# Loop entry of a cross-attention and mixture-of-experts kernel: bias add moved to VectorE, two weight chunks split in another way, one exponential and one load moved

## The chip, the cores and the metric

One core of a Trainium2 chip runs one program. The metric is the device time of that core in microseconds (us); before the change it is 419.9 us, the median of three runs (419.73 to 420.04).

## The reference, cut to what matters

```python
x = x + xattn(layernorm(x), ctx, mask)     # x: 2 x 1024 x 256; ctx: 2 x 77 x 256; 16 heads of 64
x = x + moe_ffn(layernorm(x))              # 9 experts, hidden 704, the two best of each token

def xattn(q, ctx, mask):
    qh, kh, vh = split(q @ Wq), split(ctx @ Wk), split(ctx @ Wv)
    attn = softmax(where(mask, -max, qh @ kh.T / 8))
    return merge(attn @ vh) @ Wo + bo
```

## The kernel before, in words

The 2048 tokens are 16 tiles of 128. The program has three parts: a prologue on the context alone, a loop of 16 steps (one token tile each, with later stages of earlier tiles beside it), and the experts.

**Prologue.** For each pair of heads m (8 pairs) TensorE makes keys (`keys(m)`), multiplies them with the query weights (`key_side(m)`, L554 to L564, into a ring of four PSUM banks), and makes values (`value_side(m)`, L571). ScalarE and VectorE take each result out of PSUM as a float16 part and its remainder: `a_high`/`a_low` for the key side, `v_even`/`v_odd` for the values. `key_side(m)` waits until `a_low` has read the banks that it reuses: `at_least(pe, a_lo_ok, 2 * m - 2)` (L556), so `key_side(3)` waits for both instructions of `a_low(1)`. The order of each engine's instructions is written out by hand. TensorE's is ... `key_side(2)`, `keys(7)`, `key_side(3)`, `value_side(0)`, `value_side(1)`, `key_side(4)`, `value_side(2)`, the transpose of token tile 0, and so on (L805 to L824). VectorE's begins (L1506 to L1510):

```python
a_low(0)
dve.wait_ge(xall_in[0], 16)
stats1_of(0, 2)      # statistics of token tiles 0 and 1, from x_all
aggregate1(0)
for m in range(1, 3):
    a_low(m)
```

GpSimd makes the reciprocal standard deviation of these tiles (`rstd_first`), ScalarE normalises them.

**Loads.** SyncE issues all of them from one queue in program order (L400 to L445): the context, the key weights in three parts, the first quarter of the query weights; then it waits for the second part of the key weights and issues token tiles 0 and 1 (`load_x_all(0)`, 256 KB), the second quarter of the query weights, the constants, the first half of the value weights (`load_wv(0)`, 512 KB), the rest of the query weights, the second half of the value weights, the mask, tiles 2 and 3, the bias, the output weights, three quarter-chunks of expert weights, and all other token tiles.

**Steps 0 and 1 (the loop entry).** TensorE does `scores(n)`, the transpose of tile n+1 and `make_b(g)` for g = 0, 1, 2 (step 0) and 3, 4 (step 1). `make_b` multiplies the values with Wo, so that the loop needs one product less; its ten results use PSUM banks 3 to 6 in turn, and `make_b(2)` waits until `b_low(0)` has read banks 3 and 4 (L588). For g = 0 it also adds the bias bo by a product with an identity, into the first 77 rows. ScalarE's `b_high` and VectorE's `b_low` split each result. `scores(2)` begins when `b_low(4)` is done (L749).

**Expert weights.** 36 chunks of 128 x 1088 elements go through three staging slots. `w_high(c)` on ScalarE scales a chunk in place and then casts it to float16 (two passes); `w_low(c)` on GpSimd writes the remainder. `w_direct(c)` casts and scales in one pass, and `w_rest(c)` on VectorE makes scale and remainder in one instruction; before, this pair is used for late chunks only. SyncE loads chunk c when chunk c-3 is done (L432). Its queue is in order, so `turn_x(3)` (a DMA transpose of tile 3 that needs GpSimd's `norm_low(3)`) stands ahead of `load_x(4)` and of chunks 6 and 7.

**Step 2.** ScalarE does `p_high(0)`, two `w_high`, then `normalise(4)` (which waits for `load_x(4)`), `exp(2)`, `norm_high(4)`; step 3 begins with `p_high(1)`. VectorE's `sums(2)`, `p_low(1)` and `residual(0)` follow from them, and `project(1)` on TensorE needs `residual(0)`.

Of the kernel before, what the change touches and what calls it, by code (L numbers as in the profile page):

```python
# [71 lines left out]
def build(nc, x, ctxT, mask, wq, wk, wv, wo, bo, wt, gate, gbias, consts, out):  # L72
    with ExitStack() as ctx:
# [6 lines left out]
        def sems(name, n):  # L80
            return [sem(f"{name}{k}") for k in range(n)]
# [176 lines left out]
        con_in, bc_in, ctx_in, mask_in = (sem(n) for n in ("con_in", "bc_in", "ctx_in", "mask_in"))  # L258
        wk_in, wq_in, wv_in = sems("wk_in", 3), sems("wq_in", 4), sems("wv_in", 2)
        wo_in, xall_in, half_mm, bo_in = sems("wo_in", 2), sems("xall_in", 3), sem("half_mm"), sem("bo_in")  # L260
        setup = sem("setup")
        cpy = sem("cpy")
        mask_ok = sem("mask_ok")
# [31 lines left out]
        LAG_OUT, LAG_X1, LAG_XN2, LAG_G = 2, 3, 4, 5  # L295
        W_STEP = 2
        W_PRE = 4
        WARM, WARM_IDS, WARM_HALF, WARM_OUT, WARM_X0 = 30, 28, 18, 6, 4

        X_PE = 3  # L300
# [97 lines left out]
        def _(sp):  # L398
# [15 lines left out]
            for g in range(4):  # L414
                sp.dma_start(wq_sb[:, 2 * g:2 * g + 2],
                             wq[2 * g * P:2 * (g + 1) * P].rearrange("(m p) n -> p m n", p=P)).then_inc(wq_in[g], 16)
                if g == 0:
                    sp.wait_ge(wk_in[1], 16)
                    load_x_all(0)
                if g == 1:  # L420
                    sp.dma_start(con[:], consts).then_inc(con_in, 16)
                    load_wv(0)
            load_wv(1)
            sp.dma_start(mask32, mask).then_inc(mask_in, 16)
            load_x_all(1)
# [118 lines left out]
        def _(pe):  # L544
# [41 lines left out]
            def make_b(g):  # L586

                at_least(pe, b_lo_ok, (0, 0, 2, 6, 6)[g])  # L588
                for half in range(2):
                    pe.wait_ge(wo_in[half], 16)  # L590
                    pe.wait_ge(v_half[half], PAIRS)
                even, odd = b_terms(2 * g, 0), b_terms(2 * g + 1, 1)
                if g == 0:
                    pe.wait_ge(bo_in, 16)
                rest = b_terms(2 * g, 1)
                assert len(even) == len(odd)
                for i in range(len(even)):
                    end = i == len(even) - 1
                    more = rest or g == 0
                    mm = b_product(*even[i], start=(i == 0), stop=(end and not more))  # L600
                    if end:
                        mm.then_inc(half_mm if more else b_mm, 1)
                    mm = b_product(*odd[i], start=(i == 0), stop=end)
                    if end:
                        mm.then_inc(b_mm, 1)
                    if g == 0 and end:
                        pe.wait_ge(half_mm, 1)
                        for b in range(B):
                            mm = pe.matmul(b_bank(0)[0:J, b], con[:, C_ID:C_ID + J], bo_b[:], start=False, stop=(b == B - 1),
                                           skip_group_check=True)  # L610
                        mm.then_inc(b_mm, 1)
                if rest:
                    pe.wait_ge(half_mm, 2)
                    for i in range(len(rest)):
                        mm = b_product(*rest[i], stop=(i == len(rest) - 1))
                    mm.then_inc(b_mm, 1)
# [285 lines left out]
        def _(act):  # L902
# [16 lines left out]

            def b_high(g):  # L920
                act.wait_ge(b_mm, 2 * g + 2)
                for k in (2 * g, 2 * g + 1):
                    act.activation(b_hi[:, :, B_CHUNKS[k], :], b_bank(k), ACT.Copy, scale=SP_B).then_inc(b_hi_ok, 1)

# [18 lines left out]
            def w_high(c):  # L943

                act.wait_ge(w_in[c % SLOTS], c // SLOTS * 16 + 16)
                act.activation(stage[:, c % SLOTS, :], stage[:, c % SLOTS, :], ACT.Copy, scale=SP_W).then_inc(w_sc_ok, 1)  # L946
                act.wait_ge(w_sc_ok, c + 1)
                act.activation(w_chunk(c, 0), stage[:, c % SLOTS, :], ACT.Copy).then_inc(w_hi_ok, 1)  # L948

            def w_direct(c):  # L950
# [37 lines left out]

            def step(n):
                if n == 0:  # L990
                    w_high(0)
                    x_high(1)
                    b_high(0)
                    w_high(1)
                    exp(0)
                    normalise(2)
                    b_high(1)
                    b_high(2)
                    return
                if n == 1:  # L1000
                    w_high(2)
                    x_high(2)
                    normalise(3)
                    w_high(W_PRE - 1)
                    norm_high(3)
                    b_high(3)
                    exp(1)
                    b_high(4)
                    return
                if on(n, LAG_OUT):  # L1010
                    p_high(n - LAG_OUT)
                if on(n, LAG_XN2):
                    normalise2(n - LAG_XN2)
                if n == W_STEP:
                    act.wait_ge(b_mm, NCH)
                if on_w(n) and w_place(w_at(n)) < 4:
                    act.wait_ge(stats1, NT - 3 if w_place(w_at(n)) == 0 else NT)
                if n == NT - 1:
                    gate_copy(n - LAG_G)
                if on_w(n):  # L1020
                    w_high(w_at(n))
                    w_high(w_at(n) + 1)
                if n == LAG_G:
                    act.wait_ge(zero_out, 64)
                if on(n, LAG_G) and n != NT - 1:
                    gate_copy(n - LAG_G)
                if on(n, -2):
                    normalise(n + 2)
                if n == NT - 1:
                    w_high(4 * EARLY + 2)  # L1030
                if on(n, 0):
                    exp(n)
                if on(n, -2):
                    norm_high(n + 2)
# [118 lines left out]
        def _(dve):  # L1153
# [7 lines left out]
            def v_odd(m):  # L1161
# [2 lines left out]
                dve.tensor_copy(vz[rows, m % 3, :, j0:j0 + J],  # L1164
                                ps[rows, V_BANKS[m % 3], 0:B * J].rearrange("p (b j) -> p b j", b=B)).then_inc(v_half[1], 1)

            def b_low(g):
                for k in (2 * g, 2 * g + 1):
                    c = B_CHUNKS[k]
                    dve.wait_ge(b_hi_ok, k + 1)  # L1170
                    dve.scalar_tensor_tensor(out=b_lo[:, :, c, :], in0=b_bank(k), scalar=SP_B, in1=b_hi[:, :, c, :],
                                             op0=ALU.mult, op1=ALU.subtract).then_inc(b_lo_ok, 1)
# [104 lines left out]

            def w_rest(c):

                dve.wait_ge(w_lo_ok, c)  # L1280
                dve.wait_ge(w_hi_ok, c + 1)
                dve.scalar_tensor_tensor(out=w_chunk(c, 1), in0=stage[:, c % SLOTS, :], scalar=SP_W, in1=w_chunk(c, 0),
                                         op0=ALU.mult, op1=ALU.subtract).then_inc(w_lo_ok, 1)
# [153 lines left out]
            def step(n):  # L1437
                if n == 2:
                    b_low(4)
                if on(n, 1):  # L1440
                    sums(n - 1)
                if n == 1:
                    b_low(1)
                    b_low(2)
                    dve.wait_ge(xall_in[2], 16)
                    stats1_of(4, 6)
                if on(n, LAG_OUT):
                    p_low(n - LAG_OUT)
                if on(n, LAG_X1):
                    residual(n - LAG_X1)  # L1450
                if on(n, 0):
                    maxima(n)
                if on(n, LAG_X1):
                    stats(n - LAG_X1)
                if on(n, 0):
                    shift(n)
                if on(n, LAG_X1):
                    aggregate(n - LAG_X1)
                if n in (0, 1):
                    x_low(n + 1)  # L1460
                if n == 0:
                    b_low(0)
                if n == 1:
                    b_low(3)
                    stats1_of(6, 8)
                    aggregate1(2)
                    dve.wait_ge(bc_in, 32)
                if X_PAIR <= n + 4 < NT:
                    stats1_of(n + 4, n + 5)
                if on(n, LAG_G):  # L1470
                    logits(n - LAG_G)
                    pick(n - LAG_G)
# [175 lines left out]
        def _(pool):  # L1648
# [56 lines left out]
            def step(n):  # L1705
                if on_w(n - 1):
                    w_low(w_at(n - 1) + 1)
                if n == 0:
                    w_low(0)
                    w_low(1)  # L1710
                if on(n, 1):
                    norm(n - 1)
                if n == 1:
                    w_low(2)
                    rstd_first(2)
                    w_low(W_PRE - 1)
# [122 lines left out]
```

## Time and profile before

| | |
|---|---|
| median of three runs | 419.9 us (419.73 to 420.04) |
| profiled execution | 419.24 us, its span 417.4 us |
| TensorE busy | 400.7 us (96% of the span) |
| VectorE, ScalarE, GpSimd busy | 276.3, 253.6, 253.5 us |
| chain that ended last, by engine | TensorE 52%, issue 16%, DMA 13%, VectorE 7% |

PE is TensorE's matmuls, PEld its weight loads, DVE VectorE, ACT ScalarE, POOL GpSimd, SP or SPq SyncE and its queue. Times are from the start of the span. The loop entry lies between 22.3 us and about 58 us of the span, the rest of the loop reaches to about 157 us, and the experts follow. Busy shares are averages over parts with different limits, so what the change is worth has to be read in its own stretch.

### The profile page before, as it was taken

The page shows a single profiled execution, that of the slowest core. Times are in us where ns is not written, and L with a number is a line of the kernel's source. Part 1 is how long each engine was busy: PE and PEld are TensorE (multiplying, and loading weights), DVE is VectorE, ACT ScalarE, POOL GpSimd, SP SyncE. Part 2 cuts the span into 40 slices and gives each one's busy share as a digit, 9 for nine tenths or more (in the row PEclk, how much of TensorE's full clock was granted, in tenths as well). Part 3 has the DMA queues.
Part 4 walks back from the last instruction along what each step waited for, and adds up shares of the span by engine and source line. Part 5 has one row for each costly group of instructions (what it writes and reads, how often), then busy time and mean ns, then how long its engine had stood idle before and what let it go on. Part 6 is the DMA issues. An engine that isn't in the chain of part 4 may idle for free.

```text
span 417.4 us, 10090 instructions
## 1 busy us (share of the span) xinstructions
PE 400.7 (96%) x3150; PEld 301.6 (72%) x3150; DVE 276.3 (66%) x668; ACT 253.6 (61%) x444; POOL 253.5 (61%) x214
## 2 busy tenths in 40 slices
PE   8999999999999999899999999999999999999991
PEld 7777676777777777777677777777777777777780
DVE  1777968999999999989889754434444444444330
ACT  3759789999999996735655434444444444444430
POOL 6536789999999999263345543545444444454232
PEclk9999999999999999999999999999999999999996
DMA  7993287777676787247789779999988998889842
GB/s 226 343 359 108 71 217 185 209 202 209 197 200 209 191 216 209 89 126 192 123 146 142 142 132 146 125 146 144 137 140 139 140 142 140 138 141 149 121 65 35
DMA packets 113584, 67.73 MB, mean 162 GB/s; under 512 B 88064, under 2 KB 106880, under 8 KB 113536
## 3 DMA queue, kind: packets, MB, share of 16 engines
q1 hardware_dynamic: 105856, 56.60, 59.8%
q0 software_dynamic: 7680, 10.49, 16.4%
q8 instruction: 30, 0.49, 0.5%
q14 instruction: 18, 0.15, 0.1%
HBM read 36.23 MB, written 9.96 MB: 111 GB/s over the span
## 4 chain that ended last, share of the span: by engine, by line
PE 52%; issue 16%; DMA 13%; DVE 7%; POOL 5%; POOLq 4%; ACT 2%; SPq 1%; DVEq 0%; ACTq 0%
PE ps L847 14%; PE ps L676 10%; PE ps L646 10%; DMA out_rows<-work,idx_all 9%; PE ps L867 6%; PE ps L659 3%; POOL work L1739 3%; POOLq L1748 3%; PE ps L642 2%; DMA w_all<-in_wv 2%; PE ps L583 2%; PE ps L548 1%; PE ps L691 1%; DVE work L1230 1%; DVE work L1221 1%
## 5 line engine op out<-in xcount | busy, mean ns | idle before, releaser
L847 PE MATMUL ps<-w_all,work 128*128 x960 | 150.3, 313 | 0.5 <-DVE work L1477 0.4
L847 PEld LDWEIGHTS ps<-w_all,work 128*128 128x128 f16 x960 | 93.6, 98 | 46.9 <-issue 1.2
L1760 POOL DMA_INDIRECT out_rows<-work,idx_all x40 | 64.2, 1605 | 101.4 <-ACT work L1109 91.8
L1545 DVE SCALAR_TENSOR_TENSOR work<-ps,work 128x352 f32<-128x352 f32 x80 | 41.3, 523 | 66.1 <-PE ps L847 65.9
L867 PE MATMUL ps<-w_all,work 128*128 x681 | 80.8, 273 | 0.1
L867 PEld LDWEIGHTS ps<-w_all,work 128*128 128x128 f16 x681 | 66.3, 98 | 10.8 <-issue 0.4
L1673 POOL TENSOR_TENSOR w_all<-stage,w_all 128x1088 f16<-128x1088 f32 x31 | 70.1, 2260 | 5.5 <-ACT w_all L948 5.5
L1088 ACT ACTIVATE work<-ps 128x352 f32<-128x352 f32 x80 | 36.7, 462 | 50.7 <-PE ps L847 50.7
L1094 ACT ACTIVATE work<-work 128x704 f16<-128x704 f32 x39 | 30.8, 790 | 58.5 <-DVE work L1545 58.5
L1739 POOL DMA_INDIRECT work<-xn_rows,idx_all x40 | 42.6, 1064 | 27.9 <-issue 10.4
L646 PE MATMUL ps<-w_all 128*128 128x462 f16 (+1 forms) x288 | 57.4, 336 | 0.0
L676 PE MATMUL ps<-w_all,work 128*128 128x256 f16 x320 | 53.5, 273 | 2.4 <-DVE work L1230 1.7
L646 PEld LDWEIGHTS ps<-w_all 128*128 128x128 f16 x288 | 27.9, 97 | 22.0
L676 PE MATMUL ps<-work 128*128 128x256 f16 x160 | 43.6, 273 | 0.0
L1678 POOL TENSOR_TENSOR work<-work 128x1232 f32<-128x1232 f32 x16 | 36.0, 2251 | 2.3 <-DVE work L1225 2.3
L676 PEld LDWEIGHTS ps<-w_all,work 128*128 128x128 f16 x320 | 30.4, 98 | 8.0 <-DVE work L1240 4.3
L946 ACT ACTIVATE stage<-stage 128x1088 f32<-128x1088 f32 x31 | 34.2, 1104 | 3.0 <-DMA stage<-in_wt 2.6
L948 ACT ACTIVATE w_all<-stage 128x1088 f16<-128x1088 f32 x31 | 34.4, 1111 | 1.0
L1552 DVE TENSOR_TENSOR work<-work 128x640 f16<-128x640 f32 x39 | 31.9, 818 | 0.0
L1551 DVE TENSOR_TENSOR work<-work 128x64 f16<-128x64 f32 x39 | 8.8, 227 | 30.9 <-ACT work L1094 30.8
L1221 DVE TENSOR_REDUCE work<-work 128x16 f32<-128x1232 f32 x16 | 22.8, 1423 | 7.5 <-ACT work L969 7.5
L1208 DVE TENSOR_REDUCE work<-ps 128x6 f32<-128x462 f32 (+1 forms) x48 | 25.1, 574 | 1.0 <-PE ps L646 1.0
(162 smaller groups left out, 530.5 us busy)
## 6 DMA issues: line engine op xcount, KB each, us to landing
stage<-in_wt SPq DMA_DIRECT2D x36, 544.0 KB, 4.3
work<-in_x SPq DMA_DIRECT2D x30, 128.0 KB, 2.5
out_rows<-work SPq DMA_DIRECT2D x18, 128.0 KB, 2.4
xn_rows<-work SPq DMA_DIRECT2D x18, 128.0 KB, 2.5
w_all<-in_x SPq DMA_DIRECT2D x1, 1536.0 KB, 14.1
work<-work SPq DMA_TRANSPOSE x78, 3.6
w_all<-in_wq SPq DMA_DIRECT2D x4, 256.0 KB, 6.1
w_all<-in_wv SPq DMA_DIRECT2D x2, 512.0 KB, 7.4
```

The costliest lines, as they stand in the source:

```text
L646: mm = pe.matmul(dst, lhs[:, par, k, :], rhs[:, k, b, h0 * J:h0 * J + w], start=False, stop=(k == KD - 1 and rhs is a_lo))
L676: mm = pe.matmul(ps[:, 6, 0:D], lhs[:, c, :], rhs[:, b, c, :], start=(c == 0 and n == 0), stop=(c == NCH - 1 and n == 2))
L847: mm = pe.matmul(ps[:, c, 0:half], xt[:, t % 2, block, :], weights(wbase + off, half), start=(k == 0 and n == 0), stop=(k == KD - 1 and n ...
L867: mm = pe.matmul(ps[:, Y_BANKS[t % 2], 0:D], lhs, weights(wbase + (pl * WC + W13C + c * D), D), start=(c == 0 and n == 0), stop=(c == HC - ...
L946: act.activation(stage[:, c % SLOTS, :], stage[:, c % SLOTS, :], ACT.Copy, scale=SP_W).then_inc(w_sc_ok, 1)
L948: act.activation(w_chunk(c, 0), stage[:, c % SLOTS, :], ACT.Copy).then_inc(w_hi_ok, 1)
L1088: act.activation(sg[:, t % 2, c * HID // 2:(c + 1) * HID // 2], ps[:, c, 0:HID // 2], ACT.Silu, scale=1.0 / SP_W).then_inc(silu_ok, 1)
L1545: dve.scalar_tensor_tensor(out=sg[:, t % 2, cols], in0=ps[:, 2 + c, 0:HID // 2], scalar=1.0 / SP_W, in1=sg[:, t % 2, cols], op0=ALU.mult, ...
L1673: pool.tensor_tensor(w_chunk(c, 1), stage[:, c % SLOTS, :], w_chunk(c, 0), ALU.subtract).then_inc(w_lo_ok, 1)
L1678: pool.tensor_tensor(e3, e3, rr[:, i % 2].unsqueeze(2).to_broadcast([P, HEADS, J]), ALU.mult).then_inc(norm_ok, 1)
L1739: pool.indirect_dma_start(out=xg[:, t % 2], out_offset=None, in_=xn2_rows[0:K1 * P, :] if t < NF1 else xn2_rows, in_offset=bass.IndirectOf ...
L1760: pool.indirect_dma_start(out=acc, out_offset=bass.IndirectOffsetOnAxis(ap=idx_all[:, t:t + 1], axis=0), in_=yb[:, t % 2], in_offset=None, ...
```

## The change: what it does

- The bias product on TensorE goes. VectorE adds the bias in PSUM (`add_bias`) after the first result of `make_b(0)`, and `b_high(0)` waits for it.
- Chunks 0 and 1 are split by `w_direct` on ScalarE and `w_rest` on VectorE, in place of `w_high` and `w_low`. `w_direct(1)` stands ahead of `b_high(0)`.
- In step 2 `exp(2)` stands ahead of `normalise(4)`.
- `load_x_all(0)` is issued after `load_wv(0)`; the wait ahead of it stays where it was. VectorE's order in the prologue is unchanged.

```diff
@@ sync
                 if g == 0:
                     sp.wait_ge(wk_in[1], 16)
-                    load_x_all(0)
                 if g == 1:
                     sp.dma_start(con[:], consts).then_inc(con_in, 16)
                     load_wv(0)
+                    load_x_all(0)
@@ tensor, make_b
                 even, odd = b_terms(2 * g, 0), b_terms(2 * g + 1, 1)
-                if g == 0:
-                    pe.wait_ge(bo_in, 16)
                 rest = b_terms(2 * g, 1)
                 for i in range(len(even)):
                     end = i == len(even) - 1
-                    more = rest or g == 0
-                    mm = b_product(*even[i], start=(i == 0), stop=(end and not more))
+                    mm = b_product(*even[i], start=(i == 0), stop=(end and not rest))
                     if end:
-                        mm.then_inc(half_mm if more else b_mm, 1)
+                        mm.then_inc(half_mm if rest else b_mm, 1)
                     mm = b_product(*odd[i], start=(i == 0), stop=end)
                     if end:
                         mm.then_inc(b_mm, 1)
-                    if g == 0 and end:
-                        pe.wait_ge(half_mm, 1)
-                        for b in range(B):
-                            mm = pe.matmul(b_bank(0)[0:J, b], con[:, C_ID:C_ID + J], bo_b[:], start=False, stop=(b == B - 1),
-                                           skip_group_check=True)
-                        mm.then_inc(b_mm, 1)
@@ scalar
             def b_high(g):
                 act.wait_ge(b_mm, 2 * g + 2)
+                if g == 0:
+                    act.wait_ge(bias_ok, 1)
@@ scalar, w_high
-                act.wait_ge(w_sc_ok, c + 1)
+                act.wait_ge(w_sc_ok, c + 1 - W_REST)
@@ scalar, step
                 if n == 0:
-                    w_high(0)
+                    w_direct(0)
                     x_high(1)
+                    w_direct(1)
                     b_high(0)
-                    w_high(1)
                     exp(0)
                     normalise(2)
...
+                if n == W_STEP:
+                    exp(n)
                 if on(n, -2):
                     normalise(n + 2)
...
-                if on(n, 0):
+                if on(n, 0) and n != W_STEP:
                     exp(n)
@@ vector
+            def add_bias():
+                dve.wait_ge(bo_in, 16)
+                dve.wait_ge(b_mm, 1)
+                dve.tensor_tensor(b_bank(0)[0:J], b_bank(0)[0:J], bo_b[0:J].unsqueeze(1).to_broadcast([J, B, D]),
+                                  ALU.add).then_inc(bias_ok, 1)
@@ vector, step
                 if n == 1:
+                    w_rest(1)
                     b_low(1)
                     b_low(2)
...
                 if n == 0:
+                    add_bias()
+                    w_rest(0)
                     b_low(0)
@@ gpsimd, step
-                if n == 0:
-                    w_low(0)
-                    w_low(1)
                 if on(n, 1):
                     norm(n - 1)
                 if n == 1:
+                    pool.wait_ge(w_lo_ok, W_REST)
                     w_low(2)
```

## Rows read from the trace of the kernel before

**Rows 1.** Busy time by stretch: us, then each engine's busy us, granted clock, DMA share, GB/s
```profile
22.30:58.20 35.90, 34.50 (x243) 23.63 (x240) 27.30 (x58) 28.85 (x41) 22.59 (x19) 1.00 0.59 180
58.20:154.00 95.80, 95.79 (x731) 72.63 (x732) 90.06 (x217) 91.28 (x131) 93.84 (x86) 1.00 0.72 201
```

**Rows 2.** The chain of waits that ended last: start us, us, what
```profile
7.08 6.79 DMA w_all<-in_wv
14.00 1.29 PE ps L548 x8
...
28.20 1.09 PE ps L609 x4
29.29 4.52 PE ps L583 x40
...
50.46 2.39 DMA work<-in_x
...
58.21 3.45 PE ps L676 x30
```

**Rows 3.** TensorE in order of time, key_side(3) and value_side(0): start, us, idle before
```profile
12.34 0.79 PE L560 MATMUL ps<-w_all 64*128 64x154 f32 x8
14.00 1.29 PE L548 MATMUL ps<-w_all 128*128 128x154 f32 x8 [0.87 <-DMA w_all<-in_wv]
```

**Rows 4.** VectorE in order of time: the two statistics, and a_low(1)
```profile
10.04 0.74 DVE L1177 BATCH_NORM_STATS2 st_all<-w_all 128x6 f32<-128x256 f32 x2
...
10.91 0.83 DVE L1190 TENSOR_TENSOR w_all<-ps,w_all 128x308 f16<-128x308 f32 x2
```

**Rows 5.** SyncE's issues in order of time, around the load that moves
```profile
5.64 0.37 SPq L408 DMA_DIRECT2D w_all<-in_x  x1
...
7.08 0.43 SPq L411 DMA_DIRECT2D w_all<-in_wv  x1
7.56 0.98 SPq L415 DMA_DIRECT2D w_all<-in_wq  x2
```

**Rows 6.** DMA issues of the same stretch in turn: KB, us from issue to landing
```profile
w_all<-in_x SPq DMA_DIRECT2D x1, 256.0 KB, 3.0
...
con<-in_consts SPq DMA_DIRECT2D x1, 246.0 KB, 4.8
w_all<-in_wv SPq DMA_DIRECT2D x1, 512.0 KB, 6.8
w_all<-in_wq SPq DMA_DIRECT2D x1, 256.0 KB, 7.1
```

**Rows 7.** Busy time by stretch, with the rate of all transfers at the end
```profile
10.00:15.00 5.00, 4.13 (x36) 3.29 (x33) 3.60 (x12) 2.94 (x9) 2.18 (x7) 1.00 0.98 325
```

**Rows 8.** VectorE: x_low(1), b_low(0) (two instructions), and all five w_rest
```profile
27.91 0.41 DVE L1194 TENSOR_TENSOR w_all<-ps,w_all 128x256 f16<-128x256 f32 x1
...
29.95 1.29 DVE L1171 SCALAR_TENSOR_TENSOR work<-ps,w_all 128x512 f16<-128x512 f32 x2 [1.63 <-ACT w_all L923]
L1282 DVE SCALAR_TENSOR_TENSOR w_all<-stage,w_all x5: 1279/1283/1289, 182.0 to 208.3; 128x1088 f16<-128x1088 f32 x5
```

**Rows 9.** ScalarE in order of time: b_high(0), normalise(4), the scaling pass of chunk 7
```profile
29.32 1.08 ACT L923 ACTIVATE w_all<-ps 128x512 f16<-128x512 f32 x2 [2.68 <-PE ps L609]
52.88 0.60 ACT L936 ACTIVATE work<-work,nmr_all,rstd_all 128x256 f32<-128x256 f32 x1 [2.65 <-DMA work<-in_x]
58.62 1.11 ACT L946 ACTIVATE stage<-stage 128x1088 f32<-128x1088 f32 x1 [0.34 <-DMA stage<-in_wt]
```

**Rows 10.** GpSimd in order of time: norm_low(3)
```profile
48.40 0.69 POOL L1702 TENSOR_TENSOR work<-work 128x256 f16<-128x256 f32 x1
```

**Rows 11.** TensorE's longest wait between 22 and 62 us: total, times, longest
```profile
PE ps L676 <- DVE work L1240: 0.7, 1, 0.7
```

**Rows 12.** Busy time by stretch after TensorE's last work, with the granted clock
```profile
408.30:410.60 2.30, 0.01 (x1) 0.00 (x0) 0.00 (x0) 0.47 (x1) 0.90 (x2) 1.00 0.47 57
412.00:417.40 5.40, 0.00 (x0) 0.00 (x0) 0.00 (x0) 0.00 (x0) 0.00 (x0) 0.50 0.21 24
```

More of the change, by code:

```diff
@@ L260, in build @@
         wo_in, xall_in, half_mm, bo_in = sems("wo_in", 2), sems("xall_in", 3), sem("half_mm"), sem("bo_in")
+        bias_ok = sem("bias_ok")
         setup = sem("setup")
@@ L297, in build @@
         W_PRE = 4
+        W_REST = 2
         WARM, WARM_IDS, WARM_HALF, WARM_OUT, WARM_X0 = 30, 28, 18, 6, 4
@@ L605, in make_b @@
                         mm.then_inc(b_mm, 1)
-                    if g == 0 and end:
-                        pe.wait_ge(half_mm, 1)
-                        for b in range(B):
-                            mm = pe.matmul(b_bank(0)[0:J, b], con[:, C_ID:C_ID + J], bo_b[:], start=False, stop=(b == B - 1),
-                                           skip_group_check=True)
-                        mm.then_inc(b_mm, 1)
                 if rest:
-                    pe.wait_ge(half_mm, 2)
+                    pe.wait_ge(half_mm, 1)
                     for i in range(len(rest)):
@@ L1278, in w_rest @@
             def w_rest(c):
-                dve.wait_ge(w_lo_ok, c)
+                at_least(dve, w_lo_ok, c)
                 dve.wait_ge(w_hi_ok, c + 1)
```

## The prediction, made before the changed kernel was run

> **What bounds the kernel now.** I read the busy shares by stretch first, then the chain of waits, then each engine in order of time where the change lies. From 58.2 to 154 us TensorE is busy 95.79 of 95.80 us [rows 1]: whatever reaches `project(1)`, its first work at 58.21 [rows 2], earlier or later moves the rest of the kernel by the same amount, as long as the other engines keep up. They have little room: VectorE, ScalarE and GpSimd are busy 94%, 95% and 98% of that stretch (90.06, 91.28, 93.84 of 95.80) [rows 1]. From 22.3 to 58.2 us TensorE is idle for 1.4 us [rows 1], of which one wait of 0.7 us stands at `project(1)`, for VectorE's `residual(0)` [rows 11]. Ahead of the loop it waits once more, 0.87 us for the value weights [rows 3]. So the sum to make is when `project(1)` starts after the change.
>
> **The load that moves, and who waits for it.** SyncE issues tiles 0 and 1 at 5.64, the value weights at 7.08 and the next quarter of the query weights at 7.56 [rows 5]. They land 3.0, 6.8 and 7.1 us later [rows 6], at 8.64, 13.87 (7.08 + 6.79 [rows 2]) and 14.66: in the order of issue, and from 10 to 15 us the DMA engines are 98% busy [rows 7]. After the change the value weights have 256 KB less ahead of them. The next 256 KB cost 14.66 - 13.87 = 0.8 us, so they land at about 13.1, when `key_side(3)` ends (12.34 + 0.79 = 13.13) [rows 3]. That alone would remove the 0.87 us.
>
> But the tiles now stand behind them. They have ahead of them and with them just the bytes that the value weights had before, and the issue is at the same place in the queue, so I take 13.9 us for their landing. Above, 14.7 (the place after). Below, if the transfers ran with no engine of the 16 late: the constants, one quarter of the query weights and the value weights were 246 + 256 + 512 = 1014 KB after the tiles' old landing at 8.64 [rows 6]; at 325 GB/s [rows 7] that is 3.2 us, so 11.8.
>
> The tiles' statistics are not off the path. VectorE's order is fixed: `a_low(0)` from 9.26, the two statistics from 10.04, their aggregation, and `a_low(1)` from 10.91 to 11.74 [rows 4]. The tiles were there at 8.64, 1.4 us ahead of need. Now VectorE stops ahead of the statistics until 13.9, with `a_low(1)` queued behind, and `key_side(3)` on TensorE waits for `a_low(1)` (L556). From landing to `key_side(3)` it is 11.74 - 10.04 = 1.70 us of VectorE plus two hand-overs of 0.05 us: 15.7 instead of 12.34. It takes 0.72 us (eight products in a chain; the next begins with that distance), and `value_side(0)` starts at 16.4 instead of 14.00 [rows 3]. So this edit costs 2.4 us (bounds: 0.3 with 11.8, 3.2 with 14.7; it is neutral with a landing at 11.5 and gains up to 0.87 ahead of 10.6). Everything of the prologue behind it (value sides, normalisation of tile 0, last key sides) hangs on this start and shifts with it. The mask and the later loads don't hang on it.
>
> The Trainium skill (DMA: Bandwidth & Descriptors, section Queues, rings and completion order) says that each DMA engine takes the descriptors of its ring in order, while the 16 engines finish independently. The landings in order of issue agree with it [rows 5, 6]; by it a transfer that is moved behind 512 KB can't pass them, and the sum would be the same.
>
> **Bias off TensorE.** The bias product is 1.09 us of chain, with 0.05 us ahead of it, at 28.20 [rows 2]: -1.1 us for `make_b(1)`. VectorE's add has no row. The nearest is half of `b_low` (512 elements from PSUM in 1.29 / 2 = 0.65 us [rows 8]); it could be 0.5 or 0.8, and I take 0.65.
>
> **Two chunks on VectorE.** Each `w_rest` is 1.28 us [rows 8]. In step 0 VectorE now does the bias add, 0.65, and `w_rest(0)`, 1.25, ahead of `b_low(0)`, 1.29. `x_low(1)` ended at 28.3 [rows 8]; with the shift of 2.4 it ends at 30.7, the add at 31.35, `w_rest(0)` at 32.6, `b_low(0)` at 33.9. TensorE leaves `make_b(0)` at 28.15 + 2.4 = 30.55 [rows 2] and would reach `make_b(2)` 2.7 later, at 33.3 (24 of the 40 products in the 4.52 us of [rows 2]), so it waits 0.6 us there. That is the price of these edits; with the add at nothing it would be none, and with 0.2 us more in each 1.0. `w_rest(1)` is hidden: `b_low(2)` ends near 39.1, and TensorE needs it at 39.7, behind `scores(1)`. On ScalarE `w_direct` saves two passes of 1.1 us; one lies in the wait of 2.68 us that stood ahead of `b_high(0)` [rows 9]. The other brings `exp(0)` forward, which VectorE can't use at once. GpSimd loses 4.5 us of work where it was mostly idle. At the end of `make_b(4)` the tail to `scores(2)` (`b_high(4)`, `b_low(4)`) stays; by the same walk it is 0.3 us shorter, since `sums(1)` and the statistics no longer crowd it.
>
> **The exponential.** In step 2 ScalarE waited 2.65 us for tile 4 [rows 9], which was issued at 50.46 and landed at 52.85 [rows 2], with `exp(2)` behind it; `sums(2)`, `p_low(1)` and `residual(0)` followed, and TensorE waited 0.7 us [rows 11]. With `exp(2)` ahead that wait goes: -0.7. What is late next is tile 4 itself: SyncE issues it behind `turn_x(3)`, and that waits for GpSimd's `norm_low(3)`, which ended at 49.1 [rows 10]. By the walk `b_high(3)` ends at 44.1, `b_low(3)` at 44.9, the statistics of tiles 4 to 7 at 45.8, and GpSimd is done with them, one chunk and `norm_low(3)` 4.9 us later, at 50.7: 1.6 later than before, and so are tile 4 and chunks 6 and 7. Chunk 7 already held ScalarE up for 0.34 us [rows 9]. By the walk ScalarE is 1.3 us late after chunk 7, when TensorE is 0.9 late, and `project(2)` waits 0.3 us for `residual(1)`. ScalarE has too little room to win it back.
>
> **Sum.** +2.4 (tiles) - 1.1 (bias) + 0.6 (`make_b(2)`) - 0.3 (tail) - 0.7 (exponential) + 0.3 (ScalarE) = +1.2 us. On the profiled execution, 417.4 of span and 1.8 around it, that is 419.2 + 1.2 = 420.4. The median of the runs stands 0.7 above that execution, so I expect 421.1.
>
> **Rivals.**
> *The tiles land early.* If no DMA engine is late as one was for the value weights, the landing is 11.8 and that edit costs 0.3, 2.1 less: 421.1 - 2.1 = 419.0, faster by 0.9. (Chunk 0 and tile 2 land no earlier and ScalarE would wait for them, but within the waits that TensorE has anyway.) With a landing before 10.6 it is 1.2 less again, about 418. The place is VectorE's wait ahead of the statistics; with a landing after 12.7 the change is slower than none. For it: the tiles' first transfer needed 3.0 us only, the constants 4.8. Against: the transfers at that place in the queue needed 6.8 and 7.1 [rows 6].
>
> *The clock falls in the new gap.* TensorE would be idle from 12.4 to 15.7, 3.3 us. At the end of the span the granted clock was still 1.00 (2.4 GHz) in the 2.3 us after the last product, and 0.50 (1.2 GHz) from 412 on [rows 12]. So the gap is longer than an idle time that can end at the lower level. What a fall costs has no row before the end: nothing at least, at most the 8.3 us of prologue left (14.00 to 22.34) once more; I take 1.6, since the work from 15.7 on is dense, and get 422.7. For it: the length of the gap. Against: the clock stays at 1.00 in every stretch until the end, and I can't tell how it looks at a gap with dense work on both sides.
> The Trainium skill (TensorE: Matmul & The Clock Gate, section Part 1: The HAM clock gate) says that lower level is the default, that an idle stretch brings it back, and sustained work lifts it. By that rule this change is slower than my sum; the fall after the last work agrees, and no row shows a gap of this kind.
>
> *In between.* The landing is near 12.7, or the loop entry gives back 1 us more than I walked through (`make_b(2)` doesn't wait, ScalarE catches up): 419.9 to 420.2, no change.
>
> **How the numbers follow.** Forecast 0.45 (421.1, its own range 420.5 to 422.0), clock 0.16 (422.7), early tiles 0.19 (419.0 or less), in between 0.20. Less than 0.2% (0.84 us) is about what can't be told from no change. Slower by more takes the forecast, the clock and nothing else: 0.60. No change takes the in-between case and a few of the early ones: 0.22; faster the rest, 0.18. Range 418.3 to 423.0: it takes in an early landing but not one before 10.6, and the clock's price up to 1.9.
>
> **What would show it.** (1) The tiles land at 13.9, behind the value weights at 13.1. (2) VectorE has a wait of 3.8 us on that load ahead of the statistics, and TensorE one of 3.3 us ahead of `key_side(3)`. (3) The value side starts at 16.4; the first scores 2.4 later. (4) The bias row is gone, TensorE waits about 0.6 us for `b_low` in `make_b(2)`. (5) No wait of 0.7 at `project(1)`, which starts 0.9 later than before. (6) From there both kernels run in parallel, +1.2. (7) The granted clock stays 1.00. The prediction is wrong if the statistics don't wait, or if ScalarE and VectorE, released in step 0, take back more than I found.

## The result, and the profile after

The changed kernel takes 423.36 us (median of 22 executions) against 420.65 us for the kernel before in the same rounds: ratio 1.0069, 95% interval 1.0053 to 1.0084. It is slower by 2.9 us (2.2 to 3.5). The kernel before stands 0.75 us above the 419.9 of its first three runs, from which the prediction started. The profiled execution took 421.95 us with a span of 420.1; before it was 419.24 and 417.4.

The busy times have hardly moved; the difference is in the first 20 us. The page, section 1 and the clock line of section 2, shows one digit lower than its neighbours near the start (slice 2 of 40, 10.5 to 21 us); the 7 at the end lies behind the last product:

```profile
PE 401.3 (96%) x3146; PEld 302.5 (72%) x3146; DVE 277.7 (66%) x671; ACT 251.6 (60%) x442; POOL 250.4 (60%) x212
...
PEclk9899999999999999999999999999999999999997
```

TensorE in order of time (start, us, what, idle time before it):

```profile
12.55 0.79 PE L550 MATMUL ps<-w_all 128*128 128x154 f32 x4
15.46 1.39 PE L562 MATMUL ps<-w_all 64*128 64x154 f32 x8 [2.11 <-DVE w_all L1194]
16.77 2.35 PE L550 MATMUL ps<-w_all 128*128 128x154 f32 x8
19.05 0.80 PE L562 MATMUL ps<-w_all 64*128 64x154 f32 x8
```

These are the rows that answer to [rows 3]. `key_side(3)` starts at 15.46 after 2.11 us of idleness, and then eight products of the key side take 1.39 us instead of 0.79, and the eight of two value sides 2.35 instead of 1.29. The same stretches by engine, each row ending with the granted clock, the DMA share and GB/s:

```profile
12.30:15.50 3.20, 1.09 (x12) 0.72 (x8) 1.91 (x7) 1.03 (x3) 0.58 (x3) 1.00 1.07 386
15.50:18.90 3.40, 3.40 (x16) 3.00 (x16) 1.77 (x5) 1.04 (x3) 2.78 (x3) 0.50 1.06 330
18.90:22.30 3.40, 3.40 (x30) 2.60 (x30) 2.12 (x6) 3.14 (x10) 1.40 (x1) 1.00 1.05 409
```

From 15.5 to 18.9 TensorE is busy without a break at a granted clock of 0.50 (1.2 GHz) and does 16 products; in the 3.4 us behind it, at 1.00 (2.4 GHz), it does 30. The Trainium skill (TensorE: Matmul & The Clock Gate, Part 1: The HAM clock gate) has idleness end the higher level and sustained work restore it; both are to be seen here.

VectorE shows the cause of the gap; it answers to [rows 4]:

```profile
10.19 0.87 DVE L1194 TENSOR_TENSOR w_all<-ps,w_all 128x308 f16<-128x308 f32 x2 [8.79 <-ACT w_all L898]
13.60 0.75 DVE L1181 BATCH_NORM_STATS2 st_all<-w_all 128x6 f32<-128x256 f32 x2 [2.54 <-DMA w_all<-in_x]
14.27 0.30 DVE L1186 BATCH_NORM_AGGREGATE mv_all<-st_all 128x2 f32<-128x6 f32 x2
14.48 1.60 DVE L1194 TENSOR_TENSOR w_all<-ps,w_all 128x308 f16<-128x308 f32 x4
```

The statistics stop for the tiles from 11.06 to 13.60, and `a_low(1)`, which TensorE needs, stands behind them. At the loop entry VectorE, then TensorE in `make_b(2)`, then ScalarE at chunks 6 and 7:

```profile
32.08 0.69 DVE L1168 TENSOR_TENSOR ps<-ps,bo_b 77x512 f32<-77x512 f32 x1
32.69 1.28 DVE L1286 SCALAR_TENSOR_TENSOR w_all<-stage,w_all 128x1088 f16<-128x1088 f32 x1
33.89 1.27 DVE L1175 SCALAR_TENSOR_TENSOR work<-ps,w_all 128x512 f16<-128x512 f32 x2
```
```profile
35.22 2.00 PE L585 MATMUL ps<-w_all 64*128 64x256 f32 x16 [0.65 <-DVE work L1175]
```
```profile
58.90 1.11 ACT L941 ACTIVATE stage<-stage 128x1088 f32<-128x1088 f32 x1 [0.46 <-DMA stage<-in_wt]
61.90 1.11 ACT L941 ACTIVATE stage<-stage 128x1088 f32<-128x1088 f32 x1 [0.74 <-DMA stage<-in_wt]
```

The starts of six pieces of TensorE's work in the profiled executions, in us, give the balance by stage:

| | before | after | difference |
|---|---|---|---|
| `key_side(4)` | 15.22 | 19.05 | +3.83 |
| `scores(0)` | 22.38 | 26.22 | +3.84 |
| `scores(1)` | 33.95 | 37.37 | +3.42 |
| `project(1)` | 58.21 | 60.70 | +2.49 |
| `project(2)` | 66.31 | 69.39 | +3.08 |
| first expert product | 184.45 | 187.21 | +2.76 |

The load that moved costs 3.8 us, the loop entry and the exponential give back 1.35 of it up to `project(1)`, and `project(2)` takes 0.6 of that back. The starts contain the scatter of start-up too: this execution's first key side began at 8.93, that of before at 8.00.

### The profile page after: what moved, and what is told of

It reads as the page before. It is cut to its first block, busy times and chain, and to the rows that moved or that the text cites. A ratio compares the mean times of both kernels' runs of the same rounds, so it can differ in the third digit from the quotient of the medians.

```text
span 420.1 us, 10085 instructions
## 1 busy us (share of the span) xinstructions
PE 401.3 (96%) x3146; PEld 302.5 (72%) x3146; DVE 277.7 (66%) x671; ACT 251.6 (60%) x442; POOL 250.4 (60%) x212
## 4 chain that ended last, share of the span: by engine, by line
PE 50%; issue 16%; DMA 14%; DVE 7%; POOL 6%; POOLq 3%; ACT 2%; SPq 1%; DVEq 0%; ACTq 0%
PE ps L840 14%; DMA out_rows<-work,idx_all 10%; PE ps L639 10%; PE ps L669 10%; PE ps L860 6%; PE ps L652 3%; POOL work L1744 3%; POOLq L1753 3%; PE ps L635 2%; DMA w_all<-in_x 2%; PE ps L550 1%; DMA stage<-in_wt 1%; PE ps L684 1%; POOL w_all L1680 1%; PE ps L562 1%
## 5 line engine op out<-in xcount | busy, mean ns | idle before, releaser
L1680 POOL TENSOR_TENSOR w_all<-stage,w_all 128x1088 f16<-128x1088 f32 x29 | 65.6, 2260 | 0.6 <-ACT w_all L943 0.6
L1685 POOL TENSOR_TENSOR work<-work 128x1232 f32<-128x1232 f32 x16 | 36.9, 2309 | 9.3 <-DVE work L1229 9.3
L941 ACT ACTIVATE stage<-stage 128x1088 f32<-128x1088 f32 x29 | 32.0, 1102 | 2.0 <-DMA stage<-in_wt 2.0
L943 ACT ACTIVATE w_all<-stage 128x1088 f16<-128x1088 f32 x29 | 32.2, 1111 | 0.9
## 6 DMA issues: line engine op xcount, KB each, us to landing
w_all<-in_x SPq DMA_DIRECT2D x1, 1536.0 KB, 13.9
```

The costliest lines, as they stand in the source:

```text
L1680: pool.tensor_tensor(w_chunk(c, 1), stage[:, c % SLOTS, :], w_chunk(c, 0), ALU.subtract).then_inc(w_lo_ok, 1)
L1685: pool.tensor_tensor(e3, e3, rr[:, i % 2].unsqueeze(2).to_broadcast([P, HEADS, J]), ALU.mult).then_inc(norm_ok, 1)
```

## Experiments

The theory of the loss: the late tiles stop VectorE, and with it TensorE, and on top of the delay the clock falls in the gap. Its rival: the delay is all, and the clock's share is nothing that a run can tell. A third theory, C, is about the other edits: what they win up to `project(1)` is given back at `project(2)`, because chunk 7 is late. Its rival is that they win nothing. Each group of kernels ran on one chip beside the kernel before, whose median was 421.45 (e1 to e4), 420.93 (f1 to f3 and g3), 420.89 (g1, g2, g4, h1) and 419.92 us (i1 to i4).

### The load alone, forward and back

`e1_load_back` is the changed kernel with the load where it was; `e2_load_only` the kernel before with nothing but the load moved.

```diff
 e1: in load order, g == 0
+                    load_x_all(0)
 g == 1
                     load_wv(0)
-                    load_x_all(0)
 e2: the reverse, on the kernel before
```

> The changed kernel with the load of tiles 0 and 1 back in its old place; all other edits stay. Theory A (the late tiles stop VectorE, TensorE gets a gap ahead of key_side(3), and its clock falls for 3.4 us at the end of it): no gap, clock at 1.00 in the prologue, the value side starts at 14.0 as before, and what is left of the change is a gain: faster than before by 0.8 to 1.4 us. Theory B (the loss comes from VectorE's added work in steps 0 and 1): still slower than before, by 1.5 us or more.

> The kernel before with the load of tiles 0 and 1 moved behind the value weights and nothing else. Theory A: the whole loss and more, since nothing gives back: value side 1.5 to 2.4 us later, clock at 0.50 for 3.4 us and 1.6 us for that; slower than before by 3.0 to 4.2 us. Theory B: within 1 us of before. If the clock stays up in some executions, the time is 1.6 us less in these.

Measured: e1 419.21 us, ratio 0.9946 (0.9926 to 0.9966), 2.3 us faster than before. e2 425.45, ratio 1.008 (1.0053 to 1.0108), 3.4 us slower. So the load alone turns a gain into a loss. e1's gain is larger than its trace explains (0.7 us from `scores(0)` to the experts, against 1.4 to 3.1 in the times). TensorE in e2:

```profile
16.21 1.33 PE L560 MATMUL ps<-w_all 64*128 64x154 f32 x8 [3.07 <-DVE w_all L1190]
17.47 2.41 PE L548 MATMUL ps<-w_all 128*128 128x154 f32 x8
19.80 0.40 PE L560 MATMUL ps<-w_all 64*128 64x154 f32 x2
```

It is the same picture: a wait of 3.07 us, then products at about twice their duration. e1 has neither:

```profile
13.27 0.80 PE L562 MATMUL ps<-w_all 64*128 64x154 f32 x8
13.99 1.32 PE L550 MATMUL ps<-w_all 128*128 128x154 f32 x8
```

Its chain of waits bears on theory C:

```profile
50.61 2.23 POOL w_all L1680
52.86 5.51 DMA stage<-in_wt
...
65.88 3.45 PE ps L669 x30
```

From `scores(0)` to `project(1)` e1 needs 34.49 us against 35.83 before (1.3 less), but to `project(2)` 43.48 against 43.93 (0.45 less). GpSimd's `w_low(4)` frees the buffer for chunk 7, the load takes 5.5 us, and `project(2)` hangs on ScalarE's passes behind it.

### The gap filled, and the statistics out of the way

`e3_fill_gap` puts 20 products on ones ahead of `key_side(3)`; their result is used by nothing. `e4_stats_later` takes `a_low(1)` and `a_low(2)` ahead of the statistics.

```diff
 e3, tensor
+            pe.wait_ge(k_ok, 6)
+            warm(20, WARM_BANK)
             key_side(3)
 e4, vector
-            a_low(0)
+            for m in range(3):
+                a_low(m)
             dve.wait_ge(xall_in[0], 16)
             stats1_of(0, 2)
             aggregate1(0)
-            for m in range(1, 3):
-                a_low(m)
             a_low(3)
```

> The changed kernel with 20 products of 128 columns on ones (results unused, 2.2 us) on TensorE ahead of key_side(3), where it waits for VectorE. Theory A: the clock stays at 1.00, key_side(3) and two value sides take 2.0 us instead of 3.7, and the kernel is 1.3 to 1.7 us faster than the changed one, so slower than before by 1.0 to 1.6. If the clock has no part in the loss: like the changed one, 2.7 slower than before.

> The changed kernel with VectorE's statistics of tiles 0 and 1 (and the wait for their load) behind a_low(1) and a_low(2), where the late tiles stop nobody that TensorE waits for; the load stays behind the value weights. Theory A: no gap ahead of key_side(3), clock 1.00, the value side starts at 13.2 to 13.9; the transpose of tile 0 waits up to 0.5 us; faster than before by 1.0 to 2.2 us, at least as fast as with the load back in its place. Theory B: slower than before, as with the load put back.

Measured: e3 421.97, ratio 1.0025 (1.0004 to 1.0047). Its trace:

```profile
13.52 1.28 PE L614 MATMUL ps<-onesb 128*128 128x128 bf16 x20
15.08 0.79 PE L562 MATMUL ps<-w_all 64*128 64x154 f32 x8 [0.29 <-DVE w_all L1196]
15.81 1.32 PE L550 MATMUL ps<-w_all 128*128 128x154 f32 x8
```

The products are at full speed, though `key_side(3)` starts no earlier than the tiles allow; they landed at 13.19 here, the earliest of all traces with the load late. e4 took 421.11, ratio 0.9983 (0.9961 to 1.0006), which can't be told from the kernel before; 1.0 to 2.2 us less were expected. There is no gap ahead of `key_side(3)` (14.02), but a wait of 0.72 us at the transpose of tile 0, for `normalise(0)`:

```profile
18.23 0.41 PE L623 MATMUL ps<-con,work 128*128 128x128 f32 x2 [0.72 <-ACT work L931]
```

So one order on VectorE takes back the loss, but not all of e1's gain: the rest of the prologue is written for tiles that are there.

### The exponential alone, and chunk 7 first

`f1_exp_only` is the kernel before with `exp(2)` ahead of `normalise(4)`. `f2_chunk_first` is e1 with GpSimd's `w_low(3)` ahead of `rstd_first(2)`, where GpSimd stood idle for 4.49 us in the changed kernel with that chunk queued behind. `f3_chunk_first_rest_later` is f2 with `w_rest(0)` behind `b_low(0)`, against the wait in `make_b(2)`. `g3_before_again` is the kernel before.

```diff
 f1, scalar, step 2
+                if n == W_STEP:
+                    exp(n)
...
-                if on(n, 0):
+                if on(n, 0) and n != W_STEP:
                     exp(n)
 f2, gpsimd
                     w_low(2)
-                    rstd_first(2)
                     w_low(W_PRE - 1)
+                    rstd_first(2)
 f3, vector
                     add_bias()
-                    w_rest(0)
                     b_low(0)
+                    w_rest(0)
```

> The kernel before with exp(2) ahead of normalise(4) in step 2 and nothing else. Theory as forecast: project(1) starts 0.7 us earlier and the gain stays. Theory C (the gain is given back: project(2) then waits for the chain GpSimd w_low(4), load of chunk 7, both passes of ScalarE, exp(3), residual(1), which the edit doesn't move): project(1) 0.7 earlier, project(2) 0 to 0.2 earlier, time within 0.3 us of before.

> The changed kernel with the load of tiles 0 and 1 back in its place, and on GpSimd in step 1 w_low(3) ahead of rstd_first(2), in the idle time ahead of the latter. Theory C: turn_x(3), tile 4 and w_low(4) come 1.8 to 2.2 us earlier, chunk 7 lands 1.5 us earlier, ScalarE does not wait 1.1 us for it, and project(2) starts 0.8 to 1.0 us earlier: 3.0 to 3.3 us faster than before. Without theory C (ScalarE or VectorE is full anyway): as with the load back alone, 2.2 faster.

> The last kernel, and w_rest(0) on VectorE behind b_low(0) instead of ahead of it. TensorE's wait of 0.7 us in make_b(2) goes and scores(1) start 0.6 us earlier; w_rest(0) and the load of chunk 3 come 1.2 us later. If TensorE bounds step 1, 0.4 to 0.6 us faster than the last kernel; if VectorE does (sums(0), w_rest(1), b_low(1) and b_low(2) follow in any order), the same time.

> The kernel before once more, for a second trace of it beside the runs that follow. If its time in another execution differs, both theories put it into two stretches: the prologue up to 22 us (landing of the key and value weights) and the experts; from the first scores to the first expert product the two traces agree within 0.3 us.

Measured: f1 420.63, ratio 0.9996 (0.9971 to 1.0022). Its trace reaches `project(1)` 0.84 us sooner after `scores(0)` than before and `project(2)` 0.23 sooner, with 1.2 us of waits on ScalarE for chunks 6 and 7: the exponential wins its 0.8 and gives most of it back. f2: 418.72, ratio 0.9956 (0.9936 to 0.9977). GpSimd takes the chunk first, and ScalarE goes through chunks 6 and 7 with no wait:

```profile
38.02 2.25 POOL L1680 TENSOR_TENSOR w_all<-stage,w_all 128x1088 f16<-128x1088 f32 x1 [1.64 <-ACT w_all L943]
40.85 2.26 POOL L1680 TENSOR_TENSOR w_all<-stage,w_all 128x1088 f16<-128x1088 f32 x1 [0.58 <-ACT w_all L943]
43.91 0.24 POOL L1659 TENSOR_SCALAR rstd_all<-mv_all 128x4 f32<-128x4 f32 x1 [0.80 <-DVE mv_all L1186]
```

It reaches `project(2)` 42.53 us after `scores(0)`, 1.4 less than before: nothing is given back. In the four traces with this order (f2, f3, i2, i4) `project(2)` comes 42.5 to 42.6 us after `scores(0)`, in the eight that have the other edits without it 42.7 to 43.5. So theory C holds as a mechanism, and its price differs from execution to execution. In time it is not shown: f2 is 1.9 us faster than before, e1 was 2.3, their intervals overlap, and 3.0 to 3.3 were expected. f3: 418.58, ratio 0.9937 (0.9916 to 0.9957). It reaches `scores(1)` 0.4 us sooner than f2, but `project(2)` at the same distance (42.59), so that wait was covered again; its time can't be told from f2's. g3 (420.95 us, one execution) shows how far single executions differ: its first key side starts at 10.51 instead of 8.00, `scores(0)` 1.6 us later, and from there to the experts it agrees to 0.04 us (162.03 against 162.07). That is why stages are compared from `scores(0)` on.

### The bias and the chunks alone; both kernels again

`g1_bias_only` is the kernel before with the bias edit, `g2_chunks_only` with `w_direct` and `w_rest` for chunks 0 and 1 (and without GpSimd's `w_low` for them). `g4_after_again` is the changed kernel, `h1_fill_same_chip` is e3 beside it.

```diff
 g1, vector (and the bias product on TensorE taken out)
+                    add_bias()
                     b_low(0)
 g2, scalar and vector
-                    w_high(0)
+                    w_direct(0)
                     x_high(1)
+                    w_direct(1)
                     b_high(0)
-                    w_high(1)
...
+                    w_rest(0)
                     b_low(0)
```

> The kernel before with the bias added on VectorE and nothing else. By the terms of the sum: -1.1 us on TensorE up to make_b(1); VectorE's b_low(0) stands behind the add, as before it stood behind the product, and make_b(2) needs it no later than it is there: scores(1) start 0.9 to 1.1 earlier. By theory C the gain is kept up to project(1), since the whole chain behind make_b(4) moves with it: faster by 0.6 to 1.1 us. Rival: chunk 0 or 1 or exp(0) on ScalarE hold step 1, and nothing comes out of it.

> The kernel before with chunks 0 and 1 split by w_direct and w_rest and nothing else. By the terms of the sum: make_b(2) waits for b_low(0), which stands behind w_rest(0) now: 29.3 (bias product) + b_high 1.1 + b_low 1.3 were the path before, w_rest(0) runs beside the bias product, so the wait is 0 to 0.3 us here and the edit alone gives 0 to 0.3 us, within 0.4 us of before. Rival: w_rest on VectorE costs its 1.25 us twice on the path, 1 us slower or more.

> The changed kernel once more, for a second trace and for times on the chip of the next three. Theory A: TensorE waits 1.5 to 3.5 us for a_low(1) ahead of key_side(3) again, and its clock falls again for 3.4 us in or right behind the wait; 2.5 to 3.5 us slower than before. If the fall in the first trace was chance, the clock stays at 1.00 here and the trace is 1.6 us shorter up to the first scores.

> The changed kernel with the gap filled by 20 products on ones, now on the same chip as the changed kernel itself. Theory A: 1.3 to 2.0 us faster than it, by the clock alone. If the clock costs nothing: the same time.

Measured: g1 420.08, ratio 0.9988 (0.9968 to 1.0009); `scores(0)` to `scores(1)` is 0.8 us shorter, to the experts 0.36. g2 421.19, ratio 1.0011 (0.999 to 1.0032); no stage gains over 0.3. Neither can be told from no change (0.6 to 1.1 us were expected of g1). g1's trace holds a surprise. The value weights came late there, with the loads in the order of before, and the clock fell:

```profile
15.07 2.10 PE L549 MATMUL ps<-w_all 128*128 128x154 f32 x8 [1.78 <-DMA w_all<-in_wv]
```

g4: 422.70, ratio 1.0058 (1.0029 to 1.0087), which repeats the result. Each execution lists its mean granted clock, and that separates them: four at 0.993 or 0.994 took 420.53 to 421.52 us, four at 0.988 to 0.991 took 422.11 to 423.42, four at 0.985 or 0.986 took 424.30 to 425.62. One stretch of 3.41 us at half clock lowers a mean over 420 us by 0.004, so these are most simply none, one and two such stretches; two in one execution is inferred, no trace shows it. Of the kernel before on this chip, 33 of 35 executions stand at 0.992 or more, and the two others are its slowest (422.73 and 422.82). The changed kernel had 20 of 22 and 8 of 12 below 0.992, e2 10 of 12, e3 3 of 12, e1 none of 10. Of the changed kernel's first 22, the two without a fall took 422.09 and 422.48 us, 1.4 and 1.8 above the kernel before.

h1: 422.78, ratio 1.0051 (1.0026 to 1.0076). It was expected to be 1.3 to 2.0 us faster than g4 on the same chip, and took the same time. The 20 products, expected to last 2.2 us, lasted 1.28; they left 2.32 us of idleness, and the clock fell all the same:

```profile
16.11 0.94 PE L562 MATMUL ps<-w_all 64*128 64x154 f32 x8 [2.32 <-DVE w_all L1196]
16.98 2.42 PE L550 MATMUL ps<-w_all 128*128 128x154 f32 x8
```

By the mean clock, 4 of its 12 executions lay below 0.992, against 8 of g4's. But its eight others have a median of 422.05 us, 1.0 above the four of g4 without a fall. So this pair doesn't show what the clock costs.

### A longer filling, another place, and the order that fits

`i1_fill_long` fills with 40 products. `i3_load_between` issues the tiles between the constants and the value weights. `i2_late_load_reordered` keeps the load late and moves all that uses it: `a_low(1)`, `a_low(2)` ahead of the statistics, tile 0's normalisation behind `v_even(2)`, its transposes and splits behind `key_side(5)`, and the edits of f2 and f3 on GpSimd and VectorE. `i4_best_same_chip` is f3 beside them.

```diff
 i1, tensor
+            pe.wait_ge(k_ok, 6)
+            warm(40, WARM_BANK)
             key_side(3)
 i3, load order
                     sp.dma_start(con[:], consts).then_inc(con_in, 16)
-                    load_wv(0)
                     load_x_all(0)
+                    load_wv(0)
 i2, tensor (likewise x_high(0) on ScalarE and x_low(0) on VectorE)
-            norm_turn(0)
             for m in range(5, PAIRS):
                 key_side(m)
                 value_side(m - 2)
+                if m == 5:
+                    norm_turn(0)
```

> The changed kernel with 40 products on ones ahead of key_side(3) instead of 20 (2.5 us at 2.4 GHz). Theory A: the gap that is left is under 1.5 us whenever the tiles land, the mean granted clock is 0.992 or more in at least 10 of 12 executions (20 products: 4 of 12 lay under that, the changed kernel 8 of 12), and the time is 1.0 to 1.6 us less than the changed kernel's, so slower than before by 0.8 to 1.8. If the clock is not what 20 products left: the same share of executions under 0.992 as with 20.

> The changed kernel with the load of tiles 0 and 1 issued between the constants and the value weights, 512 KB nearer. Theory A: the tiles land at 10.5 to 12.0, VectorE waits 0 to 1.2 us for them, key_side(3) starts 0 to 1.2 us late, less than the wait for the value weights that stands behind it anyway, and no fall of the clock: faster than before by 1.0 to 2.3 us, like the load back in its old place. If it is the order of issue against the key and query weights that costs: slower than before.

> The load stays behind the value weights, and the orders follow it: VectorE's statistics of tiles 0 and 1 behind a_low(2), tile 0's normalisation, transpose and split one pair of heads later on all engines, w_low(3) ahead of rstd_first(2) on GpSimd, w_rest(0) behind b_low(0) on VectorE. Theory A and C: no wait ahead of key_side(3), none at the transpose, no fall of the clock, chunk 7 in time: 2.4 to 3.2 us faster than before, and at most 0.7 faster than the next kernel, since only the wait for the value weights (0.2 to 0.9 us) is left to gain.

> The load in its old place, w_low(3) ahead of rstd_first(2), w_rest(0) behind b_low(0), once more on the chip of the last kernel, to compare the two: 2.0 to 2.8 us faster than before, no execution with a mean clock under 0.991.

Measured: i1 421.56, ratio 1.0035 (1.0021 to 1.0049), no execution below 0.992. Its trace has 1.40 us of idleness left and no fall, with `key_side(3)` at 16.41, later than in the changed kernel:

```profile
16.41 0.79 PE L562 MATMUL ps<-w_all 64*128 64x154 f32 x8 [1.40 <-DVE w_all L1196]
17.13 1.32 PE L550 MATMUL ps<-w_all 128*128 128x154 f32 x8
```

That is the delay without the clock: +1.5 us, where the changed kernel has +2.9 and +2.4. i1's interval lies below that of the changed kernel's 22 executions (1.0053 to 1.0084) and overlaps that of g4. i3: 419.39, ratio 0.9982 (0.9964 to 1.0), 0.8 us faster than before, where 1.0 to 2.3 were expected; the tiles landed at 11.29, VectorE waited 1.14 us and TensorE 0.72 ahead of `key_side(3)`. i2:

```profile
12.71 0.80 PE L562 MATMUL ps<-w_all 64*128 64x154 f32 x8
13.63 1.29 PE L550 MATMUL ps<-w_all 128*128 128x154 f32 x8
15.09 0.79 PE L562 MATMUL ps<-w_all 64*128 64x154 f32 x8 [0.17 <-issue]
```

In this trace of i2 the tiles landed at 14.24 and TensorE didn't wait for them. It took 418.23 us, ratio 0.9958 (0.9943 to 0.9973); i4 418.63, ratio 0.9966 (0.9949 to 0.9984). They are 1.8 and 1.4 us faster than before, less than the 2.4 to 3.2 and 2.0 to 2.8 expected, and can't be told from each other: once its users stand behind it, the late load shows no cost and no gain.

## Why the prediction was wrong

**What failed** is one choice: "The clock stays" was held at 0.84 and the fall at 0.16 in *The clock falls in the new gap*. The sum had the clock's price at nothing, and it measured 1.6 us. The clock fell in both traces of the changed kernel and, by the mean clock, in 28 of 34 executions. The price named there, 1.6 us, was right: `key_side(3)` and two value sides took 3.66 us (15.46 to 19.12) in place of 2.08 (0.79 and 1.29), so 1.6. The rival's 422.7 is 0.7 below the median, and that is the start of the sum, not the change: counted from 419.9 it says +2.8, and measured against 420.65 it is +2.9 (2.7 by the medians). The argument against it, that the clock stays at 1.00 in every stretch until the end, was weak: the longest idle time of TensorE between its first key side and the end is 1.54 us there (at 168), so that trace never put the question. The range's 423.0 is 3.1 above 419.9, so it had room for one fall; the median stands above it because the kernel before ran 0.75 us higher in these rounds.

**The rest by its steps.** (1) The tiles landed at 13.57 (7.26 and 6.31; 13.9 forecast), the value weights at 12.88 (13.1). (2) VectorE waited 2.54 us (3.8) and TensorE 2.11 (3.3). Both waits were shorter because this execution's key sides were 0.9 later to begin with (8.93 against 8.00); the ends that count, 15.46 for `key_side(3)` against 15.65, agree. Traces g4 and e2 show 2.95 and 3.07. (3) The value side started at 16.77 (16.4): 0.2 early, 0.6 of slow clock. (4) The add took 0.69 us (0.65), the wait in `make_b(2)` was 0.65 (0.6). (5) The wait at `project(1)` is gone. (6) `project(2)` took back 0.6 us (0.3 forecast).
From `scores(0)` on the edits sum to 2.76 - 3.84 = -1.1 us; the forecast had -1.1 + 0.6 - 0.3 - 0.7 + 0.3 = -1.2. The tiles' term without the clock is 3.83 - 1.6 = 2.2, forecast 2.4. So the sum without the clock comes to 1.1 (forecast 1.2), and the trace's +2.76 is that and the fall. That it agrees so well is partly luck: `project(2)` took back 0.3 more than forecast, and the stretch from there to the experts gave back 0.3 that was not forecast. It also varies: from `scores(0)` to the experts the same edits gain 1.4 us in g4's trace and nothing in i1's (162.12 us against 162.07 before).

**The rivals.** Early tiles did not occur: in every trace with the load late they landed between 13.2 and 14.5. What the step "ScalarE has too little room to win it back" said holds, but its price is larger, and f2 shows that it is an order on GpSimd, not room, that sets it: with that order changed, ScalarE has no wait for chunks 6 and 7.

**What stays open.** That a fall comes with the gap is shown by e1, e2, i1 and i2. Why two executions of the same kernel differ, and why 1.78 us of idleness brought a fall in g1 while 1.89 us at the second expert tile of e1 brought none, is not settled. Also e3 and h1, the same kernel, came out at 1.0025 and 1.0051. And the delay's own price is known only roughly: four executions of g4 without a fall have a median of 421.08, 0.2 us above the kernel before, while i1 is 1.5 above, h1's executions without a fall 1.2, and two of the first 22 are 1.4 and 1.8 above.

## What to carry to other kernels

- A load that moves behind another moves everything that stands behind its first user on an in-order engine. Either the users move with it (i2) or the load stays (i4).
- A new wait of TensorE can cost more than its length: here five idle gaps of 1.8 to 3.1 us in the prologue were followed by 3.4 us at half clock. That a profile shows full clock throughout says nothing of a gap that it doesn't contain.
- When a wait goes, follow the next buffer that is freed late (here chunk 7's) before counting the gain: in e1's trace 1.3 us won at `project(1)` were 0.45 at `project(2)` until one GpSimd piece of work was moved.

## What the runs showed of the hardware

- The granted clock fell after idle gaps of 1.78, 2.11, 2.32, 2.95 and 3.07 us, 0.05 to 1.1 us after the work had begun again, and for 3.41 us each time. All five gaps stand in the first 17 us. After gaps of 1.59 us (e2, at 173 us) and less it did not fall, nor after five of 1.77 to 1.90 us at 188 to 192 us (e1, e3, e4, g2, h1): length alone doesn't decide.
- In all five traces with a fall it came 10.24 us after the clock had first risen (at 5.27 us in the changed kernel, 6.08 in e2, 5.14 in g1, 6.74 in g4, 6.39 in h1), wherever the gap ended. So its moment goes with the first rise, not with the end of the gap. That may be why executions of one kernel differ; no run tests it.
- GpSimd's `norm(0)` takes 3.17 us in all 13 traces in which VectorE's `w_rest(1)`, with both operands in SBUF, runs beside it (1.07 us of overlap in the changed kernel), and 2.25 in the five without (before, g3, e2, f1, g1), where VectorE's `b_low`, which reads PSUM, runs beside it. `norm(1)` takes 2.25 to 2.26 in both kinds.

```profile
36.91 3.17 POOL L1685 TENSOR_TENSOR work<-work 128x1232 f32<-128x1232 f32 x1 [7.63 <-DVE work L1229]
```

- Landings scatter: the value weights, issued at the same place in the queue, landed at 13.87 in the trace of before, at 12.94 in e1's and at 14.94 in g1's. Start-up scatters too: the granted clock first rose at 4.5 us in the trace of before, at 10.1 in g3's, and between 4.3 and 7.0 in the others.
- The five gaps of 1.77 to 1.90 us stand at the second expert tile, with nothing that the profile shows as their cause; the other traces have less there or none. Single traces differ by up to that much for no reason of their kernel.
